# Streaming the matmul columns of a feed-forward pair in reversed order (one Trainium2 core)

## The chip, the cores and the metric

The kernel runs on one core of one Trainium2 chip. The metric is the device time of one launch in microseconds; the kernel before takes 384.68 us (median of 3 runs, 384.3 to 384.71).

## The reference

The input `x` is (8 sequences, 512 positions, 128 features) in float32. It passes through three stages, each with a residual:

```python
x = x + 0.5 * ffn(layernorm(x))
x = x + recurrence(layernorm(x))      # h = tanh(x B + h A^T) over the 512 positions, then y = h C, y @ W_out^T + b_out
x = x + 0.5 * ffn(layernorm(x))       # the same weights again

def ffn(x):                            # 128 -> 512 -> 512 -> 512 -> 128
    h = silu((x @ w1.T) * w1_s) * ((x @ w2.T) * w2_s)
    h = gelu((h @ h1.T) * h1_s)        # exact gelu
    h = gelu((h @ h2.T) * h2_s)
    return (h @ w3.T) * w3_s
```

The weights w1, w2, h1, h2 and w3 hold only -1, 0 and 1.

## The kernel before, in words

The 4096 tokens are cut into 8 chunks of 512 columns (`N` = 512 tokens, features on the 128 partitions). Both feed-forward stages walk over the 8 chunks, so there are 16 passes through layers 1 to 4; pass `g` is one turn. Within a turn the program of every engine is written out by hand, and later chunks run in hardware loops over the same turn.

Every activation is held as two float32r parts, `hi` and `lo`, and each 128x128 weight tile is multiplied with both: two matmuls of 512 columns into one PSUM bank. `split_mm` (L268 to L276) issues such a pair, and nearly all matmuls come from its line L274. Layer 1 (`layer1`) reads `xn_hi` and `xn_lo`; it has 8 output tiles (4 of w1, 4 of w2) and so 16 matmuls. Layer 2 (`layer2`) reads `y1_hi` and `y1_lo`, layer 3 (`layer3`) reads `y2_*`, each with 4 x 4 tiles and 32 matmuls. Layer 4 (`layer4`) reads `y3_*`, 4 tiles, 8 matmuls. The very first pass has versions of its own (`first_layer1`, `first_layer2`, `first_layer3`, `first_turn`), which add a low part of the weights in layer 1. These are the main passes.

Between layers, ScalarE applies tanh or gelu from PSUM (L1195, L1213, L1216), VectorE does the gating products (L807, L817) and a part of the low halves (L837, L802), and GpSimd does the rest of the low halves (L1489, L1495). All of these work column by column, with scales that belong to a partition; each waits on a semaphore that the last matmul of its output tile raises, and reads the whole 512-column bank. Layer 4's result meets the residual on VectorE (L851 for the first stage, `layer4`), and token order matters there again.

TensorE also does the transposes around the two layer norms (L282, L292, L302), the product with B (L422), the recurrence's steps (L437) and its output (L444). The change leaves these alone. While the weights load, TensorE runs 19 matmuls over zeros (L491).

The last turn cuts layer 4 in two halves of 256 columns (`last_layer4`, banks `F[1]` and `F[3]` in `B4_LAST`). The first half's result is added to the residual on VectorE and sent out while the second is computed; SyncE sends one half after the other (L1630 and L1632), and the kernel ends when the second has landed.

Of the kernel before, what the change touches and what calls it, by code (L numbers as in the profile page):

```python
# [39 lines left out]
HCOLS = CSTEPS * SCOLS  # L40
N = HALVES * HCOLS
# [4 lines left out]
KT = HID // P  # L46
# [12 lines left out]
def build(nc, xT, xtok, w1T, w2T, h1T, h2T, w3T, scales, Ablk, Brep, CTrep, WoutT, ident_d, mask_d, outT):  # L59
    with ExitStack() as ctx:  # L60
# [46 lines left out]
        w_hi = sb("w_hi", [P, WOFF[5]], F32R)  # L107
        w_lo = sb("w_lo", [P, WOFF[5]], F32R)
# [5 lines left out]
        outb = sb("outb", [P, N])  # L114
        xnt_f = sb("xnt_f", [P, N])
        xnt_m = sb("xnt_m", [P, N])
        xn_hi = sb("xn_hi", [P, N], F32R)
        xn_lo = sb("xn_lo", [P, N], F32R)
# [6 lines left out]
        y1_hi = sb("y1_hi", [P, KT, N], F32R)  # L125
        y1_lo = sb("y1_lo", [P, KT, N], F32R)
        y2_hi = sb("y2_hi", [P, KT, N], F32R)
        y2_lo = sb("y2_lo", [P, KT, N], F32R)
        y3_hi = sb("y3_hi", [P, KT, N], F32R)
        y3_lo = sb("y3_lo", [P, KT, N], F32R)  # L130
# [106 lines left out]
        def wtile(w, layer, k, m):  # L237

            width = P if layer == 4 else HID
            off = WOFF[layer] + k * width + m * P  # L240
            return w[:, off:off + P]
# [11 lines left out]
        def turned(g):  # L253

            return 0 if isinstance(g, int) and g <= 1 else g - 2

        def span(t):
            return slice(t * SCOLS, (t + 1) * SCOLS)

# [9 lines left out]
        def _(pe):  # L269
            def split_mm(out, layer, k, m, hi, lo, first, last, gen, high=True):  # L270

                pairs = ([(w_hi, hi), (w_hi, lo)] if high else []) + ([(w_lo, hi), (w_lo, lo)] if gen else [])
                for i, (w, y) in enumerate(pairs):
                    mm = nc.tensor.matmul(out, wtile(w, layer, k, m), y, start=first and i == 0,  # L274
                                          stop=last and i == len(pairs) - 1)
                return mm  # L276

# [118 lines left out]
            def last_layer4(g, r, gen):  # L396

                def part(half, ks):
                    cut = slice(half * HCOLS, (half + 1) * HCOLS)
                    for k in ks:  # L400
                        mm = split_mm(B4_LAST[half][:, cut], 4, k, 0, y3_hi[:, k, cut], y3_lo[:, k, cut], k == 0, k == KT - 1, gen)
                    return mm
                for k in range(KT - 1):
                    pe.wait_ge(y3_hi_r, 4 * g + k + 1)
                    if k == 0:
                        pe.wait_ge(y3_lo_pool, g + 1)
                    else:
                        pe.wait_ge(y3_lo_dve, (KT - 1) * g + k)
                    part(0, [k])
                    part(1, [k])  # L410
                pe.wait_ge(y3_lo_half, r + 1)
                part(0, [KT - 1]).then_inc(l4_mm_half, 1)
                pe.wait_ge(y3_lo_dve, (KT - 1) * (g + 1))
                part(1, [KT - 1]).then_inc(l4_mm, 1)
# [78 lines left out]
            def first_layer1():  # L493

                out = l1_banks(0, 0)
                w = [[wtile(part, layer, 0, 0) for part in (w_hi, w_lo)] for layer in (0, 1)]
                pe.wait_ge(w_hi_ready, 2)
                pe.wait_ge(xn_hi_r, 1)
                for b in range(2):
                    nc.tensor.matmul(out[b][:, :], w[b][0], xn_hi[:, :], start=True, stop=False)  # L500
                pe.wait_ge(w_lo1_ready, 1)
                for b in range(2):
                    nc.tensor.matmul(out[b][:, :], w[b][1], xn_hi[:, :], start=False, stop=False)
                pe.wait_ge(xn_lo_r, 1)
                for b in range(2):
                    nc.tensor.matmul(out[b][:, :], w[b][0], xn_lo[:, :], start=False, stop=False)
                    mm = nc.tensor.matmul(out[b][:, :], w[b][1], xn_lo[:, :], start=False, stop=True)
                mm.then_inc(l1_mm, 1)

            def first_layer2(k, ms=range(KT)):  # L510

                pe.wait_ge(y1_hi_r[k], 1)
                if k < KT - 1:
                    pe.wait_ge(y1_lo_r, k + 1)
                for m in ms:
                    if k == 0 and m == 2:
                        pe.wait_ge(y1_r, 3)
                    w = wtile(w_hi, 2, k, m)
                    nc.tensor.matmul(B2[m][:, :], w, y1_hi[:, k, :], start=k == 0, stop=False)  # L519
                    if k < KT - 1:  # L520
                        nc.tensor.matmul(B2[m][:, :], w, y1_lo[:, k, :], start=False, stop=False)  # L521

            def first_layer3(y, gen, *pairs):

                for k, m in pairs:
                    w = wtile(w_hi, 3, k, m)
                    low = y is y2_lo
                    mm = nc.tensor.matmul(B3_FIRST[m][:, :], w, y[:, k, :], start=k == 0 and not low,
                                          stop=k == KT - 1 and low and not gen)
                    if gen:  # L530
                        mm = nc.tensor.matmul(B3_FIRST[m][:, :], wtile(w_lo, 3, k, m), y[:, k, :], start=False,
                                              stop=k == KT - 1 and low)
                return mm

            def first_turn(gen):

                pe.wait_ge(y1_lo_last, 1)
                if gen:
                    pe.wait_ge(w_lo_ready, 1)
                for m in range(KT):  # L540
                    if gen:
                        for k in range(KT):
                            w = wtile(w_lo, 2, k, m)
                            nc.tensor.matmul(B2[m][:, :], w, y1_hi[:, k, :], start=False, stop=False)
                            nc.tensor.matmul(B2[m][:, :], w, y1_lo[:, k, :], start=False, stop=False)
                    nc.tensor.matmul(B2[m][:, :], wtile(w_hi, 2, KT - 1, m), y1_lo[:, KT - 1, :], start=False,
                                     stop=True).then_inc(l2_mm, 1)
                layer1(1, 0, gen)
                layer1(1, 1, gen)
                pe.wait_ge(w_hi_ready, len(PIECES) - 1)  # L550
                pe.wait_ge(w3_hi_ready, 1)
                pe.wait_ge(y2_hi_r, 1)
                first_layer3(y2_hi, gen, (0, 0))
                pe.wait_ge(y2_hi_r, 2)
                first_layer3(y2_hi, gen, (0, 1), (1, 0), (1, 1))
                pe.wait_ge(y2_lo_pool, 1)
                first_layer3(y2_lo, gen, (0, 0), (0, 1))
                pe.wait_ge(y2_lo_dve, 1)
                first_layer3(y2_lo, gen, (1, 0), (1, 1))
                pe.wait_ge(y2_hi_r, 3)  # L560
                first_layer3(y2_hi, gen, (2, 0), (2, 1), (0, 2), (1, 2))
                pe.wait_ge(y2_hi_r, 4)
                first_layer3(y2_hi, gen, (3, 0))
                pe.wait_ge(y2_lo_pool, 2)
                first_layer3(y2_lo, gen, (2, 0), (0, 2))
                pe.wait_ge(y2_lo_dve, 2)
                first_layer3(y2_lo, gen, (3, 0)).then_inc(l3_mm, 1)
                first_layer3(y2_lo, gen, (2, 1))
                first_layer3(y2_hi, gen, (3, 1))
                first_layer3(y2_lo, gen, (3, 1)).then_inc(l3_mm, 1)  # L570
                first_layer3(y2_hi, gen, (2, 2), (3, 2))
                first_layer3(y2_lo, gen, (1, 2), (2, 2), (3, 2)).then_inc(l3_mm, 1)
                layer1(1, 2, gen)
                first_layer3(y2_hi, gen, (0, 3), (1, 3), (2, 3), (3, 3))
                first_layer3(y2_lo, gen, (0, 3), (1, 3), (2, 3), (3, 3)).then_inc(l3_mm, 1)
                layer1(1, 3, gen)
                to_features("f", xnt_f, FR, 2)
# [182 lines left out]
        def _(dve):  # L760
# [285 lines left out]
                                        ALU.subtract).then_inc(out_sem, 1)  # L1046

            def last_layer4(half, out_sem):
                cut = slice(half * HCOLS, (half + 1) * HCOLS)
                nc.vector.scalar_tensor_tensor(out=outb[:, cut], in0=B4_LAST[half][:, cut], scalar=s3h[:, :],  # L1050
                                               in1=cols(x2_all, CHUNKS - 1)[:, cut], op0=ALU.mult, op1=ALU.add).then_inc(out_sem, 1)

# [538 lines left out]
        def _(sp):  # L1591
# [18 lines left out]
            def round_(r):  # L1610
# [16 lines left out]
                    sp.wait_ge(again_r, 1)  # L1627
                    sp.reg_load(need, again[0:1, 0:1])
                sp.wait_ge(l4_out_half, r + 1)
                sp.dma_start(outT[:, k * N:k * N + HCOLS], outb[:, 0:HCOLS]).then_inc(out_half, 16)  # L1630
                sp.wait_ge(l4_out, gb + k + CHUNKS + 1)
                sp.dma_start(outT[:, k * N + HCOLS:(k + 1) * N], outb[:, HCOLS:N]).then_inc(out_sem, 16)  # L1632

            need = sp.alloc_register("need_sp")
            round_(0)
# [46 lines left out]
```

## Time and profile before

| | before |
|---|---|
| median of 3 runs | 384.68 us |
| the profiled execution's own time | 385.06 us |
| its span, first to last instruction | 383.1 us |
| granted TensorE clock over the span | 1.00 |
| PE busy | 376.4 us, 98% |
| weight loads busy (beside the matmuls) | 300.2 us, 78% |
| VectorE, ScalarE, GpSimd busy | 73%, 70%, 43% |

A matmul's record lasts longer than the time until the next one starts, because consecutive matmuls overlap in the array. The pace of the stream is therefore read from the starts in the timeline, and not from the mean duration. PE stands for matmuls, PEld for the weight loads beside them, DVE for VectorE, ACT for ScalarE, POOL for GpSimd and SP for SyncE. L274 is line 274 of the kernel.

### The profile page before, as it was taken

How to read it: one execution, taken by the hardware profiler on the slowest of the kernel's cores; microseconds unless marked ns; L12 is line 12 of the kernel's file. 1: busy time of each engine (PE TensorE's matmuls, PEld its weight loads, DVE VectorE, ACT ScalarE, POOL GpSimd, SP SyncE). 2: the span in 40 equal slices, each digit the busy share in tenths (PEclk: the TensorE clock that was granted, in tenths of full speed). 3: DMA queues.
4: the chain of work that ended last, by engine and by line, in shares of the span. 5: the costliest groups of instructions: out<-in, count | busy, mean ns of one | idle time of the engine just before them, and what ended most of it. 6: DMA issues, size and time to landing. Idle time of an engine off the chain costs nothing.

```text
span 383.1 us, 6587 instructions
## 1 busy us (share of the span) xinstructions
PE 376.4 (98%) x1793; PEld 300.2 (78%) x1793; DVE 279.7 (73%) x724; ACT 268.0 (70%) x625; POOL 163.9 (43%) x156
## 2 busy tenths in 40 slices
PE   8999999999999999999999999999999999999995
PEld 6777777778878787878778788888888888887774
DVE  4878989896777677576868866776767677686713
ACT  3889595777858688576784767758576775757654
POOL 3555262655525355142551633525334352533421
PEclk9999999999999999999999999999999999999999
DMA  7920000000000000000001001010100101000001
GB/s 226 436 110 1 27 2 27 3 2 28 2 28 0 2 27 0 28 2 28 27 2 56 2 8 49 0 55 2 41 14 0 55 0 55 0 30 26 2 28 32
DMA packets 6365, 14.00 MB, mean 37 GB/s; under 512 B 1088, under 2 KB 2112, under 8 KB 6080
## 3 DMA queue, kind: packets, MB, share of 16 engines
q1 hardware_dynamic: 5328, 13.37, 9.1%
q10 hardware_dynamic: 1008, 0.29, 0.3%
q8 instruction: 12, 0.20, 0.2%
q14 instruction: 17, 0.14, 0.1%
HBM read 7.37 MB, written 2.10 MB: 25 GB/s over the span
## 4 chain that ended last, share of the span: by engine, by line
PE 85%; issue 7%; POOL 3%; ACT 3%; DVE 2%; POOLq 0%; DVEq 0%
PE F L274 66%; PE FR L274 7%; PE SC L491 2%; PE FR L302 2%; POOL y_lo L1489 1%; PE SC L422 1%; POOL y_lo L1495 1%; PE F L519 1%; ACT y_hi L1216 1%; PE FR L292 1%; PE SC L274 1%; PE MI L302 1%; ACT y L1213 1%; PE F L521 1%; PE MI L282 1%
## 5 line engine op out<-in xcount | busy, mean ns | idle before, releaser
L274 PE MATMUL F<-y_hi,w_hi 128*128 128x512 f32 (+1 forms) x484 | 196.6, 407 | 0.3 <-DVE y_lo L1045 0.2
L274 PE MATMUL F<-y_lo,w_hi 128*128 128x512 f32 (+1 forms) x484 | 188.6, 390 | 0.0
L274 PEld LDWEIGHTS F<-y_hi,w_hi 128*128 128x128 f32 x484 | 90.9, 188 | 20.7 <-issue 2.2
L1213 ACT ACTIVATE y<-F,sc 128x512 f32<-128x512 f32 x111 | 76.1, 686 | 41.3 <-PE F L274 40.1
L274 PEld LDWEIGHTS F<-y_lo,w_hi 128*128 128x128 f32 x484 | 91.2, 188 | 15.9
L837 DVE TENSOR_TENSOR y_lo<-y,y_hi 128x512 fp32r<-128x512 f32 x79 | 64.8, 821 | 39.2 <-ACT y_hi L1216 39.2
L1489 POOL TENSOR_TENSOR y_lo<-y,y_hi 128x512 fp32r<-128x512 f32 x48 | 66.7, 1398 | 59.1 <-DVE y_hi L824 48.5
L1495 POOL TENSOR_TENSOR y_lo<-y,y_hi 128x512 fp32r<-128x512 f32 x48 | 62.6, 1310 | 34.6 <-ACT y_hi L1216 34.4
L1216 ACT ACTIVATE y_hi<-F,sc 128x512 fp32r<-128x512 f32 x111 | 76.1, 685 | 0.0
L1232 ACT ACTIVATE h<-SC 128x32 fp32r<-128x32 f32 x96 | 18.8, 196 | 48.0 <-PE SC L437 46.8
L274 PE MATMUL F<-xn_hi,w_hi 128*128 128x512 f32 x118 | 49.5, 419 | 0.1
L807 DVE SCALAR_TENSOR_TENSOR u<-th,F 128x512 f32<-128x512 f32 x61 | 41.5, 681 | 7.0 <-ACT th L1195 7.0
L274 PE MATMUL F<-xn_lo,w_hi 128*128 128x512 f32 x118 | 46.3, 393 | 0.0
L1481 POOL TENSOR_TENSOR ve_f<-mv_f,epsc 128x4 f32<-128x4 f32 x16 | 3.2, 202 | 96.6 <-DVE mv_f L768 91.6
L817 DVE SCALAR_TENSOR_TENSOR y<-F,s12h,u 128x512 f32<-128x512 f32 x58 | 43.3, 747 | 1.6
L1195 ACT ACTIVATE th<-F,s1h 128x512 f32<-128x512 f32 x61 | 41.1, 689 | 3.2 <-PE F L274 2.4
L856 DVE TENSOR_TENSOR h<-SC,h 64x32 fp32r<-64x32 f32 x96 | 17.1, 178 | 19.0 <-ACT SC L1233 18.2
L274 PEld LDWEIGHTS F<-xn_hi,w_hi 128*128 128x128 f32 x118 | 22.1, 187 | 6.9 <-DVE y L817 1.3
L274 PEld LDWEIGHTS F<-xn_lo,w_hi 128*128 128x128 f32 x118 | 22.2, 189 | 3.4
L274 PE MATMUL FR<-y_hi,w_hi 128*128 128x512 f32 x60 | 24.0, 399 | 0.0
L274 PE MATMUL FR<-y_lo,w_hi 128*128 128x512 f32 x60 | 23.4, 390 | 0.0
L437 PEld LDWEIGHTS SC<-h,a_mix 128*128 128x128 f32 x95 | 17.8, 188 | 6.6 <-DVE h L856 2.9
(170 smaller groups left out, 439.6 us busy)
## 6 DMA issues: line engine op xcount, KB each, us to landing
x_all<-in_xT SPq DMA_DIRECT2D x1, 2048.0 KB, 16.1
x_all<-x1c SPq DMA_DIRECT2D x8, 256.0 KB, 2.3
x_all<-lnin SPq DMA_DIRECT2D x8, 256.0 KB, 2.2
out<-outb SPq DMA_DIRECT2D x7, 256.0 KB, 2.0
x_all<-in_xtok SPq DMA_DIRECT2D x1, 1536.0 KB, 12.0
w_raw<-in_h1T SPq DMA_DIRECT2D x2, 512.0 KB, 7.8
w_raw<-in_h2T SPq DMA_DIRECT2D x2, 512.0 KB, 9.3
x_all<-in_xtok SPq DMA_DIRECT2D x2, 128.0 KB, 3.2
```

Of the source, the lines that this page charges most:

```text
L274: mm = nc.tensor.matmul(out, wtile(w, layer, k, m), y, start=first and i == 0, stop=last and i == len(pairs) - 1)
L437: nc.tensor.matmul(SC[:, span(t)], a_mix[:, :], states, start=False, stop=True, skip_group_check=True).then_inc(step_mm, 1)
L807: nc.vector.scalar_tensor_tensor(out=u[:, m % 2, :], in0=th[:, m % 2, :], scalar=1.0, in1=l1_banks(g, m, late)[0][:, :], op0=ALU.add, op1= ...
L817: nc.vector.scalar_tensor_tensor(out=y1[:, m, :], in0=l1_banks(g, m, late)[1][:, :], scalar=s12h[:, m:m + 1], in1=u[:, m % 2, :], op0=ALU. ...
L837: nc.vector.tensor_tensor(y_lo[:, k, :], y[:, k, :], y_hi[:, k, :].bitcast(F32), ALU.subtract).then_inc(out_sem, 1)
L856: nc.vector.tensor_tensor(h[0:64, span(t)], SC[0:64, span(CSTEPS + t)], h[0:64, span(t)].bitcast(F32), ALU.subtract).then_inc(step_h, 1)
L1195: nc.scalar.activation(th[:, m % 2, :], l1_banks(g, m, late)[0][:, :], ACT.Tanh, scale=s1h[:, m:m + 1]).then_inc(th_r, 1)
L1213: nc.scalar.activation(y23[:, m, :], bankt[:, :], ACT.Gelu, scale=s)
L1216: nc.scalar.activation(y_hi[:, m, :], bankt[:, :], ACT.Gelu, scale=s).then_inc(hi_r, 1)
L1232: nc.scalar.activation(h[:, span(t)], SC[:, span(t)], ACT.Tanh)
L1489: pool.tensor_tensor(y1_lo[:, m, :], y1[:, m, :], y1_hi[:, m, :].bitcast(F32), ALU.subtract).then_inc(y1_lo_r if m < KT - 1 else y1_lo_las ...
L1495: pool.tensor_tensor(y_lo[:, k, :], y[:, k, :], y_hi[:, k, :].bitcast(F32), ALU.subtract).then_inc(out_sem, 1)
```

## The change

Every matmul of layers 1 to 4 reads its moving operand from the last column to the first (`t[:, ::-1]`) and writes its output columns in ascending order. One layer thus leaves its tile in reversed token order, two restore it, three reverse it again, and after layer 4 the tokens stand in their own order. The activations between the layers are elementwise, so they need no edit. Layer 4 of the last turn works in halves: the first half of the `y3` columns now holds the second half of the tokens, and so its output goes to columns 256 to 511; the residual's slice and the two output transfers follow.

```diff
+        def back(t):
+
+            return t[:, ::-1]
+
+        def mirrored(half):
+
+            return slice((1 - half) * HCOLS, (2 - half) * HCOLS)
...
@@ split_mm
-                    mm = nc.tensor.matmul(out, wtile(w, layer, k, m), y, start=first and i == 0,
+                    mm = nc.tensor.matmul(out, wtile(w, layer, k, m), back(y), start=first and i == 0,
                                           stop=last and i == len(pairs) - 1)
@@ last_layer4, on TensorE
-                        mm = split_mm(B4_LAST[half][:, cut], 4, k, 0, y3_hi[:, k, cut], y3_lo[:, k, cut], k == 0, k == KT - 1, gen)
+                        mm = split_mm(B4_LAST[half][:, mirrored(half)], 4, k, 0, y3_hi[:, k, cut], y3_lo[:, k, cut], k == 0, k == KT - 1, gen)
@@ first_layer1; first_layer2, first_layer3 and first_turn likewise
-                    nc.tensor.matmul(out[b][:, :], w[b][0], xn_hi[:, :], start=True, stop=False)
+                    nc.tensor.matmul(out[b][:, :], w[b][0], back(xn_hi), start=True, stop=False)
...
@@ last_layer4, on VectorE
-                cut = slice(half * HCOLS, (half + 1) * HCOLS)
+                cut = mirrored(half)
@@ SyncE, the last turn's output
-                sp.dma_start(outT[:, k * N:k * N + HCOLS], outb[:, 0:HCOLS]).then_inc(out_half, 16)
+                sp.dma_start(outT[:, k * N + HCOLS:(k + 1) * N], outb[:, HCOLS:N]).then_inc(out_half, 16)
                 sp.wait_ge(l4_out, gb + k + CHUNKS + 1)
-                sp.dma_start(outT[:, k * N + HCOLS:(k + 1) * N], outb[:, HCOLS:N]).then_inc(out_sem, 16)
+                sp.dma_start(outT[:, k * N:k * N + HCOLS], outb[:, 0:HCOLS]).then_inc(out_sem, 16)
```

## Rows read from the trace of the kernel before

**Rows 1.** The page: busy time per engine, share of the span, instructions; then the clock.

```profile
PE 376.4 (98%) x1793; PEld 300.2 (78%) x1793; DVE 279.7 (73%) x724; ACT 268.0 (70%) x625; POOL 163.9 (43%) x156
...
PEclk9999999999999999999999999999999999999999
```

**Rows 2.** The page, the chain that ended last, share of the span by engine.

```profile
PE 85%; issue 7%; POOL 3%; ACT 3%; DVE 2%; POOLq 0%; DVEq 0%
```

**Rows 3.** TensorE's waits: for whom, us in total, times, longest.

```profile
PE SC L491 <- DVE y_lo L1060: 1.5, 1, 1.5
PE F L500 <- ACT xn_hi L1399: 0.6, 1, 0.6
PE F L274 <- DVE y_lo L1045: 0.2, 1, 0.2
```

**Rows 4.** Windows: length, then each engine's busy us (x instructions), clock, DMA, GB/s.

```profile
200.00:240.00 40.00, 40.00 (x200) 31.86 (x199) 30.62 (x87) 26.64 (x69) 14.64 (x15) 1.00 0.07 27
...
375.00:383.10 8.10, 3.93 (x23) 3.10 (x21) 3.15 (x6) 2.64 (x6) 0.12 (x1) 1.00 0.12 36
```

**Rows 5.** PE groups by shape: source line, out<-in, shapes xcount | busy us, mean ns.

```profile
L274 PE MATMUL F<-y_hi,w_hi 128*128 128x512 f32 x476 | 194.4, 408 | 0.1
L274 PE MATMUL F<-y_lo,w_hi 128*128 128x512 f32 x476 | 186.6, 392 | 0.0
L274 PE MATMUL F<-xn_hi,w_hi 128*128 128x512 f32 x118 | 49.5, 419 | 0.1
L274 PE MATMUL F<-xn_lo,w_hi 128*128 128x512 f32 x118 | 46.3, 393 | 0.0
L274 PE MATMUL FR<-y_hi,w_hi 128*128 128x512 f32 x60 | 24.0, 399 | 0.0
L274 PE MATMUL FR<-y_lo,w_hi 128*128 128x512 f32 x60 | 23.4, 390 | 0.0
...
L274 PE MATMUL F<-y_hi,w_hi 128*128 128x256 f32 x8 | 2.2, 308 | 0.2 <-DVE y_lo L1045 0.2
```

**Rows 6.** Timeline, quiet stretch (start us, us, what); matmuls 1, 2, 17, one weight load.

```profile
365.82 0.39 PE L274 MATMUL F<-y_lo,w_hi 128*128 128x512 f32 x1
365.83 0.19 PEld L274 LDWEIGHTS F<-y_hi,w_hi 128*128 128x128 f32 x1
...
366.05 0.39 PE L274 MATMUL F<-y_hi,w_hi 128*128 128x512 f32 x1
...
369.45 0.39 PE L274 MATMUL SC<-y_lo,w_hi 128*128 128x512 f32 x1
```

**Rows 7.** Timeline of PE, slower-paced stretch; first and last of 9.

```profile
360.12 0.40 PE L274 MATMUL F<-y_hi,w_hi 128*128 128x512 f32 x1
...
361.97 0.39 PE L274 MATMUL F<-y_hi,w_hi 128*128 128x512 f32 x1
```

**Rows 8.** Timeline of PE, halves of the last turn; first and last of 11.

```profile
376.48 0.28 PE L274 MATMUL F<-y_lo,w_hi 128*128 128x256 f32 x1
...
377.68 0.28 PE L274 MATMUL F<-y_lo,w_hi 128*128 128x256 f32 x1
```

**Rows 9.** Weight loads by shape: 128, 32 and 1 columns | busy us, mean ns.

```profile
L274 PEld LDWEIGHTS F<-y_lo,w_hi 128*128 128x128 f32 x484 | 91.2, 188 | 15.9
...
L422 PEld LDWEIGHTS SC<-xn,b_rep 128*32 128x32 f32 x64 | 1.3, 108 | 2.9 <-issue 1.8 <-ACT xn L1228 1.1
...
L742 PEld LDWEIGHTS SC<-ones,ne_sum 128*1 128x1 f32 x2 | 0.1, 80 | 0.4 <-DVE ne_sum L1104 0.4
```

**Rows 10.** Timeline, the end: the last additions on VectorE, the two output transfers.

```profile
378.56 1.11 DVE L1050 SCALAR_TENSOR_TENSOR outb<-F,s3h,x_all 128x256 f32<-128x256 f32 x2
...
379.07 0.35 SPq L1630 DMA_DIRECT2D out<-outb  x1
379.70 1.70 SPq L1632 DMA_DIRECT2D out<-outb  x1
```

**Rows 11.** The page, DMA issues: KB each, median us from issue to landing.

```profile
out<-outb SPq DMA_DIRECT2D x7, 256.0 KB, 2.0
...
out<-outb SPq DMA_DIRECT2D x2, 128.0 KB, 3.1
```

More of the change, by code:

```diff
@@ L499, in first_layer1 @@
                 for b in range(2):
-                    nc.tensor.matmul(out[b][:, :], w[b][0], xn_hi[:, :], start=True, stop=False)
+                    nc.tensor.matmul(out[b][:, :], w[b][0], back(xn_hi), start=True, stop=False)
                 pe.wait_ge(w_lo1_ready, 1)
                 for b in range(2):
-                    nc.tensor.matmul(out[b][:, :], w[b][1], xn_hi[:, :], start=False, stop=False)
+                    nc.tensor.matmul(out[b][:, :], w[b][1], back(xn_hi), start=False, stop=False)
                 pe.wait_ge(xn_lo_r, 1)
                 for b in range(2):
-                    nc.tensor.matmul(out[b][:, :], w[b][0], xn_lo[:, :], start=False, stop=False)
-                    mm = nc.tensor.matmul(out[b][:, :], w[b][1], xn_lo[:, :], start=False, stop=True)
+                    nc.tensor.matmul(out[b][:, :], w[b][0], back(xn_lo), start=False, stop=False)
+                    mm = nc.tensor.matmul(out[b][:, :], w[b][1], back(xn_lo), start=False, stop=True)
                 mm.then_inc(l1_mm, 1)
@@ L518, in first_layer2 @@
                     w = wtile(w_hi, 2, k, m)
-                    nc.tensor.matmul(B2[m][:, :], w, y1_hi[:, k, :], start=k == 0, stop=False)
+                    nc.tensor.matmul(B2[m][:, :], w, back(y1_hi[:, k, :]), start=k == 0, stop=False)
                     if k < KT - 1:
-                        nc.tensor.matmul(B2[m][:, :], w, y1_lo[:, k, :], start=False, stop=False)
+                        nc.tensor.matmul(B2[m][:, :], w, back(y1_lo[:, k, :]), start=False, stop=False)
             def first_layer3(y, gen, *pairs):
@@ L527, in first_layer3 @@
                     low = y is y2_lo
-                    mm = nc.tensor.matmul(B3_FIRST[m][:, :], w, y[:, k, :], start=k == 0 and not low,
+                    mm = nc.tensor.matmul(B3_FIRST[m][:, :], w, back(y[:, k, :]), start=k == 0 and not low,
                                           stop=k == KT - 1 and low and not gen)
                     if gen:
-                        mm = nc.tensor.matmul(B3_FIRST[m][:, :], wtile(w_lo, 3, k, m), y[:, k, :], start=False,
+                        mm = nc.tensor.matmul(B3_FIRST[m][:, :], wtile(w_lo, 3, k, m), back(y[:, k, :]), start=False,
                                               stop=k == KT - 1 and low)
@@ L543, in first_turn @@
                             w = wtile(w_lo, 2, k, m)
-                            nc.tensor.matmul(B2[m][:, :], w, y1_hi[:, k, :], start=False, stop=False)
-                            nc.tensor.matmul(B2[m][:, :], w, y1_lo[:, k, :], start=False, stop=False)
-                    nc.tensor.matmul(B2[m][:, :], wtile(w_hi, 2, KT - 1, m), y1_lo[:, KT - 1, :], start=False,
+                            nc.tensor.matmul(B2[m][:, :], w, back(y1_hi[:, k, :]), start=False, stop=False)
+                            nc.tensor.matmul(B2[m][:, :], w, back(y1_lo[:, k, :]), start=False, stop=False)
+                    nc.tensor.matmul(B2[m][:, :], wtile(w_hi, 2, KT - 1, m), back(y1_lo[:, KT - 1, :]), start=False,
                                      stop=True).then_inc(l2_mm, 1)
```

## The prediction

> **What bounds the kernel now.** I read five views, in this order. The page's busy times come first: TensorE is busy for 98% of the span, the next engine for 73%, at a granted clock of full speed throughout [rows 1]. A busy share alone does not prove a bound, since overlapping matmul records can cover small gaps. The chain that ended last puts 85% of the span on TensorE [rows 2], and TensorE's own waits come to 1.5 + 0.6 + 0.2 us in the whole kernel [rows 3]. In a window of 40 us from the middle, TensorE has no idle time [rows 4]. So up to its last few microseconds the kernel is as long as its queue of matmuls. Whatever one of the reversed matmuls gains or loses is multiplied by their number and stands almost whole in the time. Only the end, 375 to 383.1 us, is something else: 3.9 us of TensorE work in 8.1 us, then VectorE and two output transfers [rows 4, 10].
>
> The number of reversed matmuls: the six large groups hold 2 x (476 + 118 + 60) = 1308 of 512 columns [rows 5]. The code gives the whole: per pass 16 + 32 + 32 + 8 = 88, over 16 passes 1408; the first pass has 16 more for the low weights in layer 1, which makes 1424; and the last layer 4 runs as 16 of 256 columns in place of 8 of 512. That leaves 1416 of 512 columns and 16 of 256.
>
> Their pace comes from start times. In the quiet stretch 16 steps take 369.45 - 365.82 = 3.63 us, 227 ns each [rows 6]. In a slower one 8 steps take 1.85 us, 231 ns each [rows 7]. I use 229 ns. The half-width ones take 1.20 us for 10 steps, 120 ns [rows 8]. The difference of the two widths gives the price of a column, (227 - 120) / 256 = 0.418 ns, and a fixed part of 227 - 512 x 0.418 = 13 ns per matmul. A column per 0.418 ns is 2.4 columns per ns, the upper of the clock's two levels (1.2 and 2.4 GHz): the array takes a column in every cycle, so for ascending float32 columns the operand read does not limit it. The 1424 equivalents times 229 ns are 326 us of the 383.1 us span.
>
> **The change part by part.**
>
> *The stream's direction.* No instruction is added or removed: 1432 matmuls keep their weights, widths, banks and waits, and only the step of the moving operand goes from +1 to -1 element. The trace of before has no row with a backward operand, so the price per column has to be bounded. The upper bound comes from the nearest row of another operand read, the weight load: 188 ns for 128 columns, 108 ns for 32, 80 ns for 1 [rows 9], so (188 - 80) / 127 = 0.85 ns per column, half the matmul's rate. It shows that TensorE has at least one read path that brings a float32 column only every second array cycle. The lower bound cannot be below the array's own cycle, so nothing is gained per column; what can be gained is the difference between the slower and the quiet stretch, 4 ns per matmul. I take 0.418 ns per column, the same as ascending, because this is the row for the same operand, the same element size and the same path into the array, and because each backward matmul reads exactly the same 2 KB per partition without gaps. Cost: 0; ends -4 x 1424 = -5.7 us and +312 us (worked out below).
>
> The price of a column is 0.418 ns with ascending columns [rows 6, 8]. The Trainium skill, "Advanced Engine Details and Errata", section SBUF Cachelines, says that SBUF is read in lines of 16 bytes, that accesses which stay in the same line run at full performance, and that a different line per access costs. A backward walk over float32 meets each line four times in a row, as the forward walk does. By this rule the sum stays at the time of before; by the weight load's row it would be 697 us. The same section says of PSUM that "any non-contiguous AP significantly slows down matmuls"; the outputs here stay ascending, so this would speak against the change only if the reader of SBUF kept a similar condition on its step. No row of this trace shows either.
>
> *The fixed part.* Each matmul pays 13 ns beside its columns [rows 6, 8]. A backward pattern starts at column 511 in place of 0. I take no change; the ends are 0 and one more such part, 13 ns x 1432 = 18.6 us.
>
> *Readers of the results.* ScalarE and VectorE wait for the last matmul of a tile, then read the whole bank. No reader starts on the first columns while later ones are written, so the order within a bank releases nobody earlier or later. Their instructions, shapes and addresses are the same; only which token sits in which column differs, and scales are per partition. Cost: 0, with nothing that has to hide it.
>
> *The last turn's halves.* TensorE still computes one half of the `y3` columns and then the other, and the output bank's half is another one. VectorE's two additions keep their 256 columns and take 1.11 us together; SyncE issues the same two transfers of 128 KB in the same places [rows 10]. The last to land is now the lower half of the columns. Same bytes and same packets, so I take 0. From the only rows for this transfer, 3.1 us for 128 KB and 2.0 us for 256 KB [rows 11], the ends are -1.1 and +1.1 us; the kernel's end waits for it, so nothing hides it.
>
> *Sum.* The profiled execution took 385.06 us: 383.1 of span and about 2.0 around it. All terms are 0, so the sum is 385.06 us. The median of the runs shown is 0.38 us lower, so I predict 384.7 us for the changed kernel.
>
> **The rivals.**
>
> *A: the backward read runs at the weight load's rate (slower).* Place: the moving operand's reader, in each of the 1432 matmuls. It decides as soon as the reader brings fewer than one column per 0.418 ns with a step of -1, since TensorE has no slack to absorb it [rows 1, 3]. Price: 512 x 0.85 + 13 = 448 ns in place of 229, so 219 x 1416 = 310 us; the halves go from 120 to 256 x 0.85 + 13 = 231 ns, 16 x 111 = 1.8 us. Time: 384.7 + 312 = 697 us. For it: the weight load proves that half rate exists on this engine [rows 9], and full rate needs two 4-byte columns per 0.84 ns, which a reader may do only for ascending neighbours. Against it: the weight load may be slow for reasons of its own, as it fills the array and doesn't stream through it. The rule of the skill about a new line per access, cited above, would belong here if a backward step made each element a new access.
>
> *B: a start cost per backward matmul (slower).* The columns stream at full rate, but the first ones come late, by up to one more fixed part: 384.7 + 18.6 = 403 us; half of that gives 394. For it: the 13 ns show that the start of a matmul is not free. Against it: weight and operand are known to the queue long before the array is free, as the weight load at 365.83 us stands 0.22 us ahead of its matmul at 366.05 [rows 6], so a start delay of the read has cover if the operand is fetched as early.
>
> *C: the slower stretches become quiet (faster).* The paces of 227 and 231 ns under different work on the other engines [rows 6, 7] could come from SBUF or PSUM accesses that collide with the stream, and a reversed order moves these. If half of the 1424 lose 4 ns, the time is 384.7 - 2.8 = 381.9 us. For it: the two paces exist. Against it: nothing in the profile ties them to the order of columns, and a collision may as well be made as removed.
>
> *D: the change does not do what it says.* The pattern could be issued as ascending, with reversed results only by accident of four layers. The time would be 384.7 us too, so it adds nothing to the numbers; it shares the first case.
>
> **How the numbers follow.** The forecast, with D in it, gets 0.74: the row of the same operand speaks for it, and its own range is 383.9 to 385.5 us, which is 0.2% to either side. That is about what a measurement of this kernel tells from no change. A gets 0.13, as the half-rate path is shown by a row but for another operand; B gets 0.07, C 0.06. Faster by over 0.2% is C, 0.06; within 0.2% is 0.74; slower is A and B, 0.20. For a range that holds 8 times in 10 I take in C fully, so the low end is 381.8, and the nearer part of B, up to about 5 us or 4 ns per matmul, so the high end is 390. A and the rest of B, 0.17 together, stay outside: taking A in would mean a range to 697 with nothing between.
>
> **What would show each step right or wrong.** If the forecast holds, the starts of the L274 matmuls in a quiet stretch of the changed kernel stand 227 ns apart, the halves at the end 120 ns, and the mean durations of the six large groups stay between 390 and 419 ns. Under A the starts stand near 448 ns, the durations grow by about 220 ns, the busy shares of ScalarE and VectorE fall to some 40% (268 and 280 us in 695), and the clock stays at full speed. Under B starts move by 5 to 13 ns in both widths alike, the half-width ones included; a cost per column would move them in proportion to the width. Under C the slow stretches near 231 ns disappear while the quiet ones stay. The transfer at the end is checked by its time to landing beside 3.1 us. The prediction is wrong if the backward operand has any price per column, since even 0.01 ns per column adds 0.01 x 512 x 1424 = 7.3 us.

## The result: 1.0% slower

The changed kernel takes 388.37 us (median of 4 runs, 387.64 to 388.56), the one before 384.49 us in the same comparison. The ratio is 1.0101 with a 95% interval of 1.0082 to 1.0119. A second comparison gave 1.0093 (1.0076 to 1.011). The range of 381.8 to 390 us holds the time, but the likeliest case, no change, is wrong: it is slower by 3.9 us.

The page of the changed kernel (span, busy us and share per engine, the chain that ended last by engine) shows a longer TensorE:

```profile
span 386.6 us, 6587 instructions
...
PE 380.1 (98%) x1793; PEld 301.0 (78%) x1793; DVE 278.6 (72%) x724; ACT 268.1 (69%) x625; POOL 162.4 (42%) x156
...
PE 98%; ACT 0%; DVE 0%; issue 0%
```

The number of instructions is the same, TensorE is busy 3.7 us longer than in [rows 1], and no other engine works more than 0.1 us longer. The chain that ended last lies on TensorE for 98% of the span, against 85% in [rows 2]; since TensorE waited no longer before than now, that difference is no sign of another bound. TensorE's waits (for whom, us in total, times, longest) are those of [rows 3] to the tenth:

```profile
PE SC L499 <- DVE y_lo L1068: 1.5, 1, 1.5
PE F L508 <- ACT xn_hi L1407: 0.6, 1, 0.6
PE F L282 <- DVE y_lo L1053: 0.2, 1, 0.2
```

Windows of the changed kernel (columns as in [rows 4]): the one from the middle has no idle time, as before. The mean clock of the last one is 0.95, which is (1 - 0.95) / 0.5 x 11.6 = 1.2 us at the lower level (1.2 GHz); the last matmul starts at 382.24 us and is over by then, so none runs at it.

```profile
200.00:240.00 40.00, 40.00 (x199) 31.85 (x198) 29.47 (x85) 27.20 (x71) 15.35 (x15) 1.00 0.07 27
375.00:386.60 11.60, 7.29 (x37) 5.75 (x36) 3.19 (x6) 5.17 (x10) 1.28 (x1) 0.95 0.09 27
```

The timeline of the changed kernel's TensorE (start us, us, what), around the two small matmuls (one column each) that stand before the last turn, and on into the quiet stretch of [rows 6]:

```profile
362.52 0.19 PE L699 MATMUL MI<-ones,h_nes 128*1 128x1 f32 x2
362.64 0.51 PE L282 MATMUL F<-y_hi,w_hi 128*128 128x512 f32 x1
362.98 0.40 PE L282 MATMUL F<-y_lo,w_hi 128*128 128x512 f32 x1
363.22 0.40 PE L282 MATMUL F<-y_hi,w_hi 128*128 128x512 f32 x1
...
365.08 0.40 PE L282 MATMUL F<-y_hi,w_hi 128*128 128x512 f32 x1
...
366.02 0.40 PE L282 MATMUL F<-y_hi,w_hi 128*128 128x512 f32 x1
...
369.75 0.40 PE L282 MATMUL F<-y_hi,w_hi 128*128 128x512 f32 x1
```

From 366.02 to 369.75 us there are 16 steps in 3.73 us, 233 ns each; the quiet stretch of before had 227 [rows 6]. Right behind the small ones, 8 steps from 363.22 to 365.08 take 1.86 us, 233 ns again; there the kernel before needed 231 [rows 7]. So the changed kernel has one pace, 233 ns, where the kernel before had two. Over all 1416 matmuls of 512 columns, the time from each start to the next sums to 340.0 us before and 344.4 us after, +3.1 ns each. That sum holds the steps in which TensorE waits and those next to a small matmul as well. By place, with steps of up to 0.26 us alone: from the second to the ninth matmul behind a small one the mean step was 230.6 ns and is 233.6 (733 steps in each trace); from the tenth on it was 227.8 and is 233.4 (392 and 395 steps).

The smaller matmuls take 0.5 us less in sum, since some start earlier behind a 512-column one, so the stream from the first real matmul to the last grew by 3.9 us. The first real matmul stands at 9.49 us in place of 10.00, because the 19 matmuls over zeros took less time:

```profile
1.47 7.48 PE L491 MATMUL SC<-y_lo 128*128 128x512 f32 x19 [1.47 <-DVE y_lo L1060]
1.47 6.98 PE L499 MATMUL SC<-y_lo 128*128 128x512 f32 x19 [1.47 <-DVE y_lo L1068]
```

Their starts stand 427 ns apart, a column per cycle of the lower clock level (1.2 GHz), up to 7.61 us before the change and up to 6.33 us in this execution, and from then on about 230 ns. So this part has nothing to do with the stream's direction. With 0.1 us more at the end this gives the span's +3.5 us.

The halves of the last turn (first and last of 11 starts, as in [rows 8]) and the transfers at the end:

```profile
379.85 0.28 PE L282 MATMUL F<-y_lo,w_hi 128*128 128x256 f32 x1
...
381.03 0.28 PE L282 MATMUL F<-y_lo,w_hi 128*128 128x256 f32 x1
...
382.43 0.35 SPq L1638 DMA_DIRECT2D out<-outb  x1
...
383.07 1.84 SPq L1640 DMA_DIRECT2D out<-outb  x1
```

Ten backward steps of 256 columns take 1.18 us, 118 ns each, where ascending took 120. The backward read costs nothing at this width. The two transfers take 3.2 us from issue to landing, against 3.1 [rows 11].

### The profile page after: what moved, and what is told of

It reads as the page before. It is cut to its first block, busy times and chain, and to the rows that moved or that the text cites. A ratio compares the mean times of both kernels' runs of the same rounds, so it can differ in the third digit from the quotient of the medians.

```text
span 386.6 us, 6587 instructions
## 1 busy us (share of the span) xinstructions
PE 380.1 (98%) x1793; PEld 301.0 (78%) x1793; DVE 278.6 (72%) x724; ACT 268.1 (69%) x625; POOL 162.4 (42%) x156
## 4 chain that ended last, share of the span: by engine, by line
PE 98%; ACT 0%; DVE 0%; issue 0%
PE F L282 75%; PE FR L282 8%; PE FR L310 2%; PE F L536 2%; PE SC L499 2%; PE SC L430 1%; PE F L527 1%; PE SC L282 1%; PE MI L310 1%; PE MI L290 1%; PE FR L300 1%; PE F L529 1%; PE SC L445 1%; PE MI L452 0%; PE MI L282 0%; PE F L554 0%
## 5 line engine op out<-in xcount | busy, mean ns | idle before, releaser
L282 PE MATMUL F<-y_hi,w_hi 128*128 128x512 f32 (+1 forms) x484 | 199.0, 412 | 0.3 <-DVE y_lo L1053 0.2
L282 PE MATMUL F<-y_lo,w_hi 128*128 128x512 f32 (+1 forms) x484 | 191.2, 396 | 0.0
L845 DVE TENSOR_TENSOR y_lo<-y,y_hi 128x512 fp32r<-128x512 f32 x79 | 63.2, 799 | 41.4 <-ACT y_hi L1224 40.5
L1497 POOL TENSOR_TENSOR y_lo<-y,y_hi 128x512 fp32r<-128x512 f32 x48 | 65.8, 1374 | 60.2 <-DVE y_hi L832 48.9
L1503 POOL TENSOR_TENSOR y_lo<-y,y_hi 128x512 fp32r<-128x512 f32 x48 | 62.1, 1299 | 36.0 <-ACT y_hi L1224 35.8
```

Source lines behind the costliest of these rows:

```text
L282: mm = nc.tensor.matmul(out, wtile(w, layer, k, m), back(y), start=first and i == 0, stop=last and i == len(pairs) - 1)
L845: nc.vector.tensor_tensor(y_lo[:, k, :], y[:, k, :], y_hi[:, k, :].bitcast(F32), ALU.subtract).then_inc(out_sem, 1)
L1497: pool.tensor_tensor(y1_lo[:, m, :], y1[:, m, :], y1_hi[:, m, :].bitcast(F32), ALU.subtract).then_inc(y1_lo_r if m < KT - 1 else y1_lo_las ...
L1503: pool.tensor_tensor(y_lo[:, k, :], y[:, k, :], y_hi[:, k, :].bitcast(F32), ALU.subtract).then_inc(out_sem, 1)
```

## The experiments

Two kinds of kernel were run. A *stream kernel* only issues groups of 24 matmuls, each group behind a 32-column matmul, with all other engines idle and the rest of the computation left out; every group has one line, `nc.tensor.matmul(bank, weights, operand)`, and differs in the operand's pattern. The *full kernels* are the changed one with another `back`.

**1. Ascending and descending alone, by width and by start.**

```python
y[:, i % 8, 0:512]                                   # L54   ascending
y[:, i % 8, 0:512][:, ::-1]                          # L59   descending
y[:, i % 8, 1:513]                                   # L69   ascending from element 1
y[:, i % 8, 0:512].rearrange("p (a b) -> p a b", b=4)[:, ::-1, :]   # L134
y[:, i % 8, 0:512].rearrange("p (a b) -> p a b", b=4)[:, :, ::-1]   # L139
y[:, i % 8, 0:1024:2]                                # L149  every second element
```

> This kernel only streams: 22 groups of 24 float32r matmuls with ScalarE, VectorE and GpSimd idle; the feed-forward pair and the recurrence are left out, its output is the input. Theory 1 (a fixed cost at each backward matmul): ascending 512 columns start every 226 to 227 ns, descending 512 every 233 ns, and at 448 and 384 columns the difference is again 6 to 7 ns. Theory 2 (a cost per backward column): the difference shrinks with the width, 5.8 ns at 448, 5 ns at 384. Theory 3 (the cost belongs to where a stream starts within a 16-byte line, not to its direction): ascending from element 1 or 3 costs 233 ns too, and a descending stream that starts on the first element of a line costs another amount than one that starts on the last. Theory 4 (the loss comes from meeting the other engines' accesses): ascending and descending are equal here. At 256 columns both are near 119 ns, as the weight load of 128 columns is then the longer of the two. With a 32-column matmul before every sixth, ascending falls to 229 to 231 ns on the steps that are not next to it and descending stays at 233.

The timeline of this kernel merges equal neighbours; a row gives the start, the us to the end of the last, and the count. A matmul's own record is 0.39 to 0.40 us (0.64 in L149), so the step is (us - 0.39) / (count - 1). First the first nine of the ascending and the descending group, then the last twelve of several groups (thirteen of L149):

```profile
25.28 2.33 PE L54 MATMUL B<-y,w 128*128 128x512 f32 x9
...
30.88 2.35 PE L59 MATMUL B<-y,w 128*128 128x512 f32 x9
...
27.91 2.88 PE L54 MATMUL B<-y,w 128*128 128x512 f32 x12
33.54 2.96 PE L59 MATMUL B<-y,w 128*128 128x512 f32 x12
44.89 3.00 PE L69 MATMUL B<-y,w 128*128 128x512 f32 x12
105.56 2.96 PE L134 MATMUL B<-y,w 128*128 128x512 f32 x12
111.22 2.88 PE L139 MATMUL B<-y,w 128*128 128x512 f32 x12
124.39 6.08 PE L149 MATMUL B<-y,w 128*128 128x512 f32 x13
```

Ascending ends at 227 ns a step and descending at 233, with no other engine at work, so theory 4 (meeting the other engines) falls. The two paces of the kernel before are here too: an ascending group starts with 233, 236, 224, 231, 236, 228, 233, 231 ns behind its first matmul (the row of nine: (2.33 - 0.39 - 0.32) / 7 = 231, without the first step of 0.32) and then stays at 227. So [rows 7] was not slowed by ScalarE or VectorE; it stands right behind a small matmul. A descending stream never reaches 227.

Groups of four columns in descending order with ascending insides (L134) cost 233 ns; the same groups ascending with descending insides (L139) cost 227. Four float32 columns are 16 bytes. What costs is the order of the 16-byte groups, not that of the elements in them. An ascending stream from element 1 (L69) costs 237 ns, and one from element 3 costs 229, so the start's place matters as well, as theory 3 said, but it does not explain the aligned case. Every second element (L149) takes (6.08 - 0.64) / 12 = 453 ns, twice as long for twice as many 16-byte groups; in descending order it takes 466.

By width, ascending against descending: 203 and 207 ns at 448 columns, 173 and 178 at 384, 147 and 147 at 320, 120 and 118 at 256. It is neither a fixed price per matmul (theory 1) nor clean per column (theory 2): it goes to nothing at 320.

**2. Which layers.**

```diff
-    mm = nc.tensor.matmul(out, wtile(w, layer, k, m), back(y), ...
+    mm = nc.tensor.matmul(out, wtile(w, layer, k, m), back(y) if layer in (2, 3) else y, ...   # and the first pass likewise
```

> Only layers 2 and 3 read backward (1024 of the 1416 matmuls of 512 columns), layers 1 and 4 ascend, the last turn's halves stand as in the kernel before. If each backward matmul costs on average 3 to 4 ns wherever it stands: 1024 / 1424 of the 3.9 us, so +2.8 us, 387.3 us. If the cost sits in layer 1 and 4 (or in the last turn's exchange): no more than +1.1 us, 385.6 us.

> Only layers 1 and 4 read backward (392 matmuls of 512 columns and 16 of 256), with the last turn's halves exchanged as in the change. If each backward matmul costs the same wherever it stands: 392 / 1424 of 3.9 us, so +1.1 us, 385.6 us. If the exchange of halves at the end or layer 1's place on the path were the cause: +2 us or more.

Layers 2 and 3 alone: 387.27 us, ratio 1.0088 (1.0074 to 1.0102), +3.3 us. Layers 1 and 4 alone: 385.84 us, ratio 1.0046 (1.0032 to 1.0059), +1.9 us. Layers 2 and 3 come near their share by number (2.8 us were expected). Layers 1 and 4 come out above theirs (1.1 us) and near the "+2 us or more" that was expected if the exchange of halves at the end were the cause. It is not: the halves' steps are no longer than before, and down_by_64 below, which exchanges the halves too, has the time of the kernel before. The two parts add up to more than the change itself (5.2 against 3.9 us). Their traces show where the excess arises: in layers_1_4_only the first ascending matmul behind a descending one takes 238 ns and the next 232 (means of 26 places), then 227; in layers_2_3_only the second descending one behind ascending ones takes 240. So each change of direction costs some 6 to 16 ns more. It is not so for every mixture: in the first stream kernel, one ascending and one descending matmul in turn came to 230 ns (L84), the mean of the two paces, but to 233 where both read the same tile (L89).

**3. Elements or 16-byte groups, in the full kernel.**

```diff
 def back(t):
-    return t[:, ::-1]
+    return t.rearrange("p (a b) -> p a b", b=4)[:, ::-1, :]     # lines_down
+    return t.rearrange("p (a b) -> p a b", b=4)[:, :, ::-1]     # inside_fours, halves not exchanged
```

> The full kernel; groups of four columns are read in descending order, the four inside ascend. Theory L: as slow as the change, 233 ns per matmul, 388 us. Theory E: as the kernel before, 384 us.

> The full kernel; groups of four columns ascend, the four inside are read in descending order; the last turn's halves stand as in the kernel before. Theory E: as slow as the change. Theory L: no loss. Beyond that, if the kernel before loses time in the matmuls that follow each small matmul (231 ns in place of 227 for eight or nine of them), this order saves some 20 to 33 ns at each of 137 places: 3 to 4 us, so 380 to 381 us, with the mean step of 512-column matmuls at 227 to 228 ns in place of 229.6.

> The change itself beside the other two on one chip: 388 us, ratio 1.010.

lines_down takes 387.97 us, ratio 1.010 (1.0081 to 1.0119); the change beside it 387.95 us, 1.0093 (1.0076 to 1.011); inside_fours 384.12 us, 0.9998 (0.9986 to 1.0011). The quiet stretch of inside_fours (first and last of 17 starts) has the pace of the kernel before, 3.62 us in 16 steps:

```profile
363.91 0.39 PE L282 MATMUL F<-y_lo,w_hi 128*128 128x512 f32 x1
...
367.53 0.39 PE L282 MATMUL F<-y_lo,w_hi 128*128 128x512 f32 x1
```

Theory L holds and theory E falls. The expected gain of 3 to 4 us did not come: the mean step is 229.7 ns, as before. The first stream kernel had reached 227 ns after three matmuls in this order, in place of nine; in the full kernel the second to ninth matmul behind a small one take 230.7 ns, as before.

**4. How many steps down it takes.**

```python
r(b, sel) = y[:, i % 8, 0:512].rearrange("p (a b) -> p a b", b=b) + sel
r(b, [:, ::-1, :])   # b = 4, 8, 16, 32, 64, 128: L99, L104, L109, L114, L119, L124
r(b, [:, :, ::-1])   # b = 4, 2, 8, 16, 64, 256:  L64, L69, L79, L84, L89, L94
```

> Only streams again, groups of 24 matmuls of 512 columns, each group behind a 32-column matmul, the other engines idle; the rest of the computation is left out. Theory L (the cost comes from stepping down from one 16-byte line, four float32 columns, to the one before it, 127 times in a stream): blocks of 4, 8, 16, 32, 64, 128 in descending order with ascending insides cost less the fewer steps down they have, 233 ns at 4, near 230 at 8, 227 from 16 or 32 on; blocks of 8, 16, 64 or 256 ascending with descending insides cost more the longer the descending run is. Theory E (the cost belongs to descending elements): twos and fours that descend inside cost 233 ns as well; the first table speaks against it with 227 ns for fours. One weight tile or one accumulating bank changes neither 227 nor 233 ns. The start of a group: ascending takes about nine matmuls at 231 ns on average before it is steady at 227, descending inside fours takes two.

Here `r` is only a shorthand for the operand. The last twelve matmuls of some of these groups (reading as above):

```profile
102.37 2.88 PE L119 MATMUL B<-y,w 128*128 128x512 f32 x12
96.70 2.96 PE L114 MATMUL B<-y,w 128*128 128x512 f32 x12
79.56 2.96 PE L99 MATMUL B<-y,w 128*128 128x512 f32 x12
61.97 3.37 PE L84 MATMUL B<-y,w 128*128 128x512 f32 x12
124.86 2.88 PE L139 MATMUL B<-y,w 128*128 128x512 f32 x12
130.49 2.96 PE L144 MATMUL B<-y,w 128*128 128x512 f32 x12
```

Seven steps down (blocks of 64, L119) cost nothing; 15 steps (blocks of 32, L114) cost 233 ns, alternating between 229 and 238; 31, 63 and 127 steps (L99) cost the same 233. So it is not a price per step down: the stream falls from one steady pace to another. One pattern is far worse: blocks of 16 ascending with descending insides (L84) take (3.37 - 0.43) / 11 = 267 ns, though a fully descending stream takes 233. Its neighbours do not: blocks of 8, 64 and 256 with descending insides take 233 ns, and blocks of 32 (in the next stream kernel) 237. One weight tile, or one accumulating bank (L139 ascending, L144 descending), leave both paces as they are. But ascending in one bank settles after three matmuls in place of nine. Groups that are interrupted by a small matmul before every sixth show no gain for fours descending inside: 23 matmuls and four small ones take 5.75 us from first to last start, and 5.76 us in ascending order. Behind one of these interruptions the ascending stream runs at 227 ns from its second matmul on, and behind two others at 231. So the time that a stream takes to settle is not fixed by its order, and inside_fours gained nothing; what fixes it was not found.

```diff
+    return t.rearrange("p (a b) -> p a b", b=64)[:, ::-1, :]    # down_by_64
+    return t.rearrange("p (a b) -> p a b", b=16)[:, :, ::-1]    # inside_sixteens
```

> The full kernel; 8 blocks of 64 columns in descending order, ascending inside. The stream table gave 227 ns for this order, so the time of the kernel before, 384 us. If any reversal of a stream's ends cost time in the kernel (another tile's last columns first, a mirrored last turn), 388 us as the change.

> The full kernel; blocks of 16 columns ascend, the 16 inside are read in descending order. The stream table gave 267 ns for this order, 37 ns above the kernel's mean of 229.6. If the price of the order passes into the kernel one for one: 37 x 1416 = 52 us, so 436 us, with the engines behind TensorE waiting more. If part of it found slack, clearly less.

down_by_64 takes 384.24 us, ratio 0.9995 (0.9983 to 1.0006), though it exchanges the halves and reads every tile's end first. inside_sixteens takes 431.48 us, ratio 1.1228 (1.1206 to 1.125), +47.2 us. Its timeline (consecutive starts) has the 267 ns of the stream kernel:

```profile
368.19 0.43 PE L282 MATMUL F<-y_hi,w_hi 128*128 128x512 f32 x1
368.45 0.43 PE L282 MATMUL F<-y_lo,w_hi 128*128 128x512 f32 x1
368.72 0.43 PE L282 MATMUL F<-y_hi,w_hi 128*128 128x512 f32 x1
368.99 0.43 PE L282 MATMUL F<-y_lo,w_hi 128*128 128x512 f32 x1
369.25 0.43 PE L282 MATMUL F<-y_hi,w_hi 128*128 128x512 f32 x1
```

The pace of the stream kernel passes into the full kernel, a little under the expected 52 us. From the second matmul behind a small one on, the mean step grows by the expected 37 ns (229.7 to 266.7); the first one takes 313 ns in the kernel before and 339 here, only 26 more.

**5. What the reader is limited by.**

```python
wt(i)[:, 0:32] ...                                   # L79 ascending, L84 descending: weights of 32 columns
yb[:, i % 4, 0:512], yb[...][:, ::-1]                # L139, L144: bfloat16, ascending and descending
yb[:, i % 4, 0:1024:2]                               # L149: bfloat16, every second element
```

> Only streams, groups of 24 matmuls, other engines idle; the rest of the computation is left out. Known: ascending 227 ns, descending 233 ns at 512 columns. Theory W (the descending read meets the weight load that runs beside it): with weights of 64 or 32 columns, whose load is shorter, descending loses less or nothing. Theory R (it is the moving operand's own reader that needs the time): 233 ns at any weight width. Theory H (a fixed price at each hand-over from one stream to the next): at 480 and 416 columns descending is 6 to 7 ns above ascending, at 352 too; if the price grows with the columns read, it falls from 6.7 at 512 towards 0 at 320. Halving the partitions changes nothing. An output written descending is a separate matter: if PSUM were sensitive to it, its ascending stream would be slower than 227 ns. In bf16 a line of 16 bytes holds eight columns: under theory R descending bf16 loses less than 6 ns or nothing, and step 2 does not halve the rate as it did in float32 (454 ns). Blocks of 16 with descending insides come out near 267 ns again, blocks of 32 between 233 and 267.

The last eleven or twelve matmuls of these groups (a record alone is 0.38 to 0.40 us):

```profile
118.37 2.54 PE L139 MATMUL B<-yb,wb 128*128 128x512 bf16 x11
123.38 2.75 PE L144 MATMUL B<-yb,wb 128*128 128x512 bf16 x12
128.94 2.65 PE L149 MATMUL B<-yb,wb 128*128 128x512 bf16 x11
55.88 2.94 PE L79 MATMUL B<-y,w 128*32 128x512 f32 x12
61.48 2.96 PE L84 MATMUL B<-y,w 128*32 128x512 f32 x12
```

In bfloat16, operand and weights alike, both directions take 216 ns, (2.54 - 0.38) / 10 and (2.75 - 0.38) / 11. With every second element, four columns per 16 bytes as in float32, bfloat16 takes 226 ns. So 512 columns out of 64 groups of 16 bytes take 216 ns, out of 128 groups 226 to 227, and out of 256 groups 453 (L149 of the first stream kernel). At 128 and at 256 groups that is 1.77 ns a group. This fits a reader of 16-byte groups that begins to be the limit at four columns a group: direction matters there (233 against 227) and at two columns a group (466 against 453), and not at eight. But it is an inference: between 320 and 512 columns the ascending step grows by (227 - 147) / 192 = 0.417 ns a column, the array's cycle of the prediction, and only the descending one grows faster, (233 - 162) / 160 = 0.44 ns from 352 columns on.

Weights of 32 columns still give 233 ns descending (L84), and so do weights of 64, so the shorter weight load does not help the descending stream, and theory W falls in the main. The gap between the directions shrinks all the same, since the ascending stream gets slower: it takes 230 ns with weights of 64 columns and 231 with 32 (L79), and never settles at 227. An output written descending leaves 227 and 233 ns as they are, and so do 64 partitions. Theory H falls again: 217 and 220 ns at 480 columns, 188 and 191 at 416, 160 and 162 at 352.

**6. A version that reads fewer 16-byte groups.** The finding suggests bfloat16 for the low halves. From the kernel before, for layer 4 in every pass and for the other layers from pass 3 on:

```diff
-    pairs = ([(w_hi, hi), (w_hi, lo)] if high else []) + ([(w_lo, hi), (w_lo, lo)] if gen else [])
+    pairs = [(w_hi, hi), (w_bf, lo)] + ([(w_lo, hi)] if gen else [])      # low halves written as bfloat16
...
+    pool.tensor_copy(w_bf[:, i * HID:(i + 1) * HID], w_hi[...].bitcast(F32)).then_inc(w_bf_ready, 1)   # 11 pieces
```

> The kernel before (all streams ascending) with the low halves of the activations, and a copy of the weights for them, in bfloat16 from pass 3 on (for layer 4 from the first pass): 13 x 44 + 12 = 584 matmuls of 512 columns read 64 lines of 16 bytes in place of 128. GpSimd makes the copy of the weights in 11 pieces during the first three turns. If the float32 streams are limited by the lines they read (step 227 to 233 ns) and a bfloat16 stream by the array (216 ns): 584 x 11 to 14 ns = 6.4 to 8.2 us less, 376 to 378 us. If the step belongs to the hand-over between streams of any type, or if changing the type at each matmul costs as much: 384 us. If GpSimd's extra work delays the low halves of the first turns: some of the gain is lost at 20 to 60 us, where TensorE would show idle time.

It took 1654.8 us. TensorE has 6929 instructions in place of 1793, and one of its waits (columns as above) tells why:

```profile
PE SC L458 <- DVE h_first L894: 20.2, 6, 3.7
```

The kernel ends after one round of the second stage only if two states of the recurrence agree bit for bit; else it runs six rounds more, and here the restart was waited for six times. Where both kinds alternate, a pair of one float32r and one bfloat16 matmul takes 460 ns (starts of neighbouring pairs at 202.28 and 202.74 us), about as long as two float32r ones; the two paces alone would give 443. The last run kept the first stage as it was and grouped the types:

```diff
+    for out, layer, k, m, hi, lo, first, last in parts:     # four high halves,
+        nc.tensor.matmul(out, wtile(w_hi, layer, k, m), hi, start=first, stop=False)
...
+    for out, layer, k, m, hi, lo, first, last in parts:     # then four low ones
+        mm = nc.tensor.matmul(out, wtile(w_bf, layer, k, m), lo, start=False, stop=last)
```

> The kernel before with the low halves of layers 1 to 3 in bfloat16 in the second feed-forward stage only (passes 8 to 15), so that the recurrence sees bit-identical inputs and ends after one round as in the kernel before; and there, apart from the first output tile of layers 2 and 3, all high halves of an output tile come before all low ones, which gives 2 changes of type per 8 matmuls in place of 8. The last kernel's trace shows a pair of one float32r and one bfloat16 matmul in 460 ns (202.28 to 202.74 us), as much as two float32r ones, where 227 + 216 = 443 were expected: so a change of type costs about 8 ns each. Theory T (a price per change of type): a tile of 8 matmuls takes 4 x 227 + 4 x 216 + 17 = 1789 ns in place of 1837; 48 tiles save 2.3 us, the 32 calls of layer 1 another 0.5 us, together 381 us. Theory A (the bfloat16 gain exists only in streams of one type for long): no gain or a loss, 384 to 385 us.

386.03 us, ratio 1.004 (1.0027 to 1.0053). It ended after one round, so the extra rounds did come from the first stage's changed bits. Two windows and one wait of it:

```profile
40.00:80.00 40.00, 37.35 (x175) 28.83 (x174) 33.92 (x91) 27.55 (x50) 24.52 (x29) 1.00 0.04 14
...
PE F L296 <- POOL y_lo L1555: 2.0, 2, 1.0
```

TensorE is idle for 2.65 us between 40 and 80 us (0.17 before), and 2.0 us of its waits are for low halves that GpSimd makes. GpSimd is busy for 24.52 us of that window in place of 20.26, as it copies the weights there. In the second stage a turn takes 22.39 us against 22.50 before (starts of the same piece in two neighbouring turns), so about 0.9 us is gained over 8 turns; theory T had 2.8, and neither theory the loss at 40 to 80 us. Neither bfloat16 version beats the kernel before, and no other run is clear of it on the fast side.

## Why the forecast missed and its range held

The range holds the time, but that is luck as far as the mechanism goes. Its upper end came from B, a cost at the start of every backward matmul, cut at about 4 ns; what came was another mechanism whose price, 3.1 ns, happens to lie below that. The forecast itself, no change with 0.74, missed.

- *What bounds the kernel, and the count of matmuls*: right. TensorE has no slack, and 1416 times the change of the step, 4.4 us, stands in the time but for 0.5 us that the smaller matmuls give back.
- *The stream's direction, taken at a cost of 0*: this is the step that failed. It rested on "for ascending float32 columns the operand read does not limit it", and took the backward column at the ascending price of 0.418 ns. The runs show 233 ns in place of 227 for a descending stream with nothing else running, and 3.1 ns per matmul in the kernel. The row "for the same operand" spoke only for ascending order, and the slope between two widths does not show how near its limit the reader is. Nor are the remaining 13 ns a mere start cost of any matmul: 512 columns take 216 ns in bfloat16 and 226 in bfloat16 with every second element, so 10 of them come with twice as many 16-byte groups. That a reader at its limit has no reserve for a less convenient order is the likeliest reading of this, not a shown one.
- *Its own sign of being wrong*, "any price per column", was set too wide: 3.1 ns on 512 columns are 0.006 ns per column, and it is no price per column, as 320 and 256 columns lose nothing.
- *The rivals.* A, the weight load's rate, did not come: 233 ns against 448. B had the sign and, in the upper range, the size (13 ns at most; 6.7 in a steady stream), but not the mechanism: it asked for equal steps at both widths, and 256 columns lose nothing. Over the whole kernel it is only 3.1 ns, since the kernel before ran at 231 and not at 227 behind its small matmuls, which stand in 137 places.
- *C, the slower stretches.* Its reading of [rows 7] as collisions with other engines was wrong: the two paces stand in a stream with all other engines idle, and in the kernel the slower one stands at the start of a stream behind a small matmul.
- *Readers of the results, the halves, the last transfers*: right, 0 within 0.1 us. The transfer of 128 KB takes 3.2 us to land against 3.1, and down_by_64, which exchanges the halves too, has the time of before.
- *The Trainium skill*, "Advanced Engine Details and Errata", section SBUF Cachelines: the trace agrees with the first half of the rule, since the order within four float32 columns is free (227 ns, 384.12 us). The conclusion drawn from it, that a backward walk meets each line four times and so costs nothing, is refuted by 233 ns for float32; in bfloat16, where a line holds eight columns, it holds (216 ns in both directions). The rule says nothing of the order of the lines. The sentence on PSUM that the prediction quotes beside it stands in the section PSUM Cachelines; no run here bears on it but the descending output, which cost nothing.

What stays open: what in the read makes descending order slower, why the pace is held at 233 ns at all numbers of steps down from 15 to 127, why descending insides of 16 take 267, and what decides when an ascending stream settles at 227, which it never does with weights of 64 and 32 columns. No run looks into the reader.

## What to carry to other kernels

Where TensorE is the bound and the operand is float32, read it in ascending order of 16-byte groups. Four columns may be reversed inside, and blocks of 64 columns or more may stand in descending order, at no cost; a full reversal costs 6 ns of 227 per matmul, and the worst pattern tried 40. At 320 and 256 columns, and in bfloat16 at 512, direction cost nothing. Read the pace from start times, and compare a second element type before a column price is called the array's own. A pattern's price can be measured in a kernel that only streams, and passes into the full kernel almost one for one (267 ns gave +47 us of an expected 52). Its settling does not: the quick start of one order in the stream kernel was not there in the full one.

## What was not expected of the hardware

- A float32r stream behind a small matmul mostly runs some eight matmuls at 231 ns before it settles at 227, with nothing else running. The kernel before spends about 2 us on this (733 steps at 230.6 in place of 227.8).
- With weights of 32 columns in place of 128 the ascending stream is slower, 231 against 227 ns, though the weight load is shorter.
- Every second float32 element halves the rate (453 ns); every second bfloat16 element costs only 10 ns more (226 against 216).
- Changes between float32r and bfloat16 matmuls cost more than bfloat16 saves: a pair takes 460 ns in place of 443, two float32r ones 454.
- At 256 columns descending is slightly faster than ascending, 118 against 120 ns.
